# Expert loop of a mixture-of-experts block: three banks for up, two results in one bank, outputs copied by VectorE

## What is computed

```python
logits = jnp.einsum('th,eh->te', x, gate_w)
scores = jax.nn.softmax(logits, axis=-1)
topk_w, topk_idx = jax.lax.top_k(scores, K)                      # K = 2, E = 16
combine = jnp.sum(jax.nn.one_hot(topk_idx, E, dtype=x.dtype) * topk_w[..., None], axis=1)
gu = jnp.einsum('th,ehj->etj', x, w_gate_up)                     # H = 256, 2 * I = 352
h = _swiglu(gu, I)                                               # silu(g) * u
y = jnp.einsum('eti,eih,te->th', h, w_down, combine)
y = y + _swiglu(x @ shared_gate_up, SI) @ shared_down            # SI = 352
```

## Time and profile before

| | us |
|---|---|
| median of 3 runs (lowest, highest) | 277.54 (276.98, 279.88) |
| the profiled execution's own time | 279.51 |
| its span, first to last instruction | 277.7 |
| mean granted clock of TensorE, share of full | 0.981 |
| TensorE busy with matmuls, share of the span | 247.9, 89% |
| VectorE, ScalarE, GpSimd busy | 152.3, 125.7, 92.2 |

### The profile page before, as it was taken

The page is one execution under the profiler, slowest core; times in us unless marked ns, Lnnn a source line. Parts: engine busy times, 40 slices in busy tenths (PEclk is TensorE's granted clock), DMA queues, the critical chain, the costliest instruction groups (busy, mean ns, idle before and its releaser), DMA issues.

```text
span 277.7 us, 4961 instructions
## 1 busy us (share of the span) xinstructions
PE 247.9 (89%) x1518; PEld 173.9 (63%) x1518; DVE 152.3 (55%) x460; ACT 125.7 (45%) x461; POOL 92.2 (33%) x106
## 2 busy tenths in 40 slices
PE   3799899898989999988789999899988998798995
PEld 2455565565555667676668787567755765475784
DVE  1636658878888766535797598452202213121274
ACT  1164867759595778910334225033314323233430
POOL 2110110111111201011552005647566575575471
PEclk9999999999999999999799999999997999979999
DMA  7999977100000800000004000322232232333394
GB/s 216 267 333 372 333 173 182 54 2 1 1 2 3 294 1 4 0 2 0 0 4 145 4 0 5 96 76 83 89 94 67 84 97 78 94 79 77 99 362 162
DMA packets 20706, 28.02 MB, mean 101 GB/s; under 512 B 2688, under 2 KB 17674, under 8 KB 20682
## 3 DMA queue, kind: packets, MB, share of 16 engines
q1 hardware_dynamic: 16395, 18.71, 22.1%
q0 software_dynamic: 2976, 8.13, 10.1%
q10 hardware_dynamic: 1311, 0.88, 1.1%
HBM read 21.55 MB, written 6.16 MB: 100 GB/s over the span
## 4 chain that ended last, share of the span: by engine, by line
PE 69%; DVE 10%; issue 6%; ACT 6%; DMA 4%; another core or an unknown queue 3%; SPq 1%; POOL 0%; ACTq 0%; DVEq 0%; POOLq 0%
PE bank L874 14%; PE bank L886 8%; PE bank L805 8%; PE bank L547 5%; PE bank L506 5%; ACT pr_s L983 4%; PE bank L537 3%; DMA x_s<-in_x 3%; PE bank L559 3%; PE bank L582 3%; PE bank L865 3%; PE bank L855 2%; PE bank L528 2%; DVE kbd L1217 2%
## 5 line engine op out<-in xcount | busy, mean ns | idle before, releaser
L983 ACT ACTIVATE pr_s<-bank,mx 128x128 f32<-128x128 f32 x128 | 46.7, 421 | 2.6 <-DVE mx L1207 2.6
L874 PE MATMUL bank<-gu_s,bxT 128*128 x124 | 44.3, 483 | 1.9 <-DVE bxT L1520 1.7
L1526 DVE TENSOR_TENSOR pr_s<-bank,pr_s 128x176 f32<-128x176 f32 x31 | 10.6, 341 | 61.7 <-ACT pr_s L1146 47.0
L464 POOL DMA_INDIRECT expert_out<-by,prT x31 | 32.0, 1032 | 26.5 <-ACT by L973 20.5
L973 ACT ACTIVATE prT<-bank 128x512 f32<-128x512 f32 (+1 forms) x63 | 32.8, 521 | 16.9 <-PE bank L547 11.2
L459 POOL DMA_INDIRECT qx_s<-ffn_in,prT x31 | 30.1, 972 | 14.6 <-issue 9.3
L983 ACT ACTIVATION_READ_ACCUMULATOR pr_s<-bank,mx 128x1 f32 x128 | 33.6, 263 | 0.0
L886 PE MATMUL bank<-dn_s,prT 88*128 x124 | 32.5, 386 | 0.1
L874 PEld LDWEIGHTS bank<-gu_s,bxT 128*128 128x128 f32 x124 | 21.9, 196 | 10.4 <-issue 4.0
L973 ACT ACTIVATE by<-bank 128x256 f32<-128x256 f32 x31 | 11.9, 385 | 26.2 <-PE bank L886 10.9
L547 PE MATMUL bank<-tab,pr_s 128*128 128x128 f32 x128 | 20.2, 280 | 3.9 <-ACT pr_s L983 2.6
(11 more groups left out here) (186 smaller groups left out, 422.4 us busy)
## 6 DMA issues: line engine op xcount, KB each, us to landing
gu_s<-in_w_gu SPq DMA_DIRECT2D x8, 704.0 KB, 9.2
dn_s<-in_w_dn SPq DMA_DIRECT2D x4, 704.0 KB
qx_s<-in_ctx_in SPq DMA_DIRECT2D x2, 512.0 KB, 9.8
ffn_in<-x_s SPq DMA_DIRECT2D x4, 256.0 KB, 2.6
cv_s<-expert_out SPq DMA_DIRECT2D x4, 256.0 KB, 3.3
x_s<-expert_out SPq DMA_DIRECT2D x4, 256.0 KB, 4.8
out<-x_s SPq DMA_DIRECT2D x7, 128.0 KB
gu_s<-in_x_t SPq DMA_DIRECT2D x1, 768.0 KB, 12.1
```

Of the source, the lines that this page charges most:

```text
L464: pool.indirect_dma_start(expert_out[:], bass.IndirectOffsetOnAxis(ap=idx[:, 1, k:k + 1], axis=0), by[:, k % RB, :], None).then_inc(dma_sc ...
L874: last = mm(bank[2 + i % 2][:, 0:2 * I], bxT[:, i % 2, k, :], gu_s[:, k, bass.ds(e, 1), :], start=k == 0, stop=k == KD - 1)
L983: last = nc.scalar.activation(pr_s[:, n % 2, h, :], score_bank(n)[:, h * T:(h + 1) * T], ACT.Exp, bias=mx[:, n % 4, h:h + 1], accum_out=de ...
```

## The change

The loop is skewed by one block more. TensorE's iteration i is now hidden_transpose(i-3), expert_up(i), block_transpose(i+3), expert_down(i-4). Up has three banks (2, 3, 5) in place of two, the turned products keep two. The turned rows and the outputs share three banks (6, 7, 4), the rows in the first 256 columns and the outputs in the last 256: bank i mod 3 gets block_transpose(i+3) and then expert_down(i-4), and VectorE reads both after that. So bT_out(i+3) waits for expert_down(i-4) as well, block_transpose for the y_out of the outputs that were in its bank, and expert_down for bT_out. The turned rows (now blT, carved from prT), bh and bhT have three copies; bs has two still. y_out moves from ScalarE's list to VectorE's, behind h_mul(i) and bT_out(i+3); its last four stand ahead of weigh_pair(0). GpSimd's scatter is ten blocks behind its gather in place of eight. The last pair's shared matmuls use banks 5, 3, 5 in place of 5, 7, 6. Six registers hold expert numbers in place of four.

```diff
@@ -291,8 +292,12 @@
-        shared_bank = lambda q, c: bank[((6, 7, 1) if q < PAIRS - 1 else (5, 7, 6))[c]]
+        shared_bank = lambda q, c: bank[((6, 7, 1) if q < PAIRS - 1 else (5, 3, 5))[c]]
...
+        expert_bank = lambda i: bank[(2, 3, 5)[i % 3]]
+        row_bank = lambda i: bank[(6, 7, 4)[i % 3]]
+        out_rows = lambda i: row_bank(i + 7)[:, D:2 * D]
...
@@ -314,8 +319,9 @@
-        bh = carve(prr, 2 * I).rearrange("p (r n) -> p r n", r=2)
-        bhT = carve(ptr, 4 * T)[0:IH, :].rearrange("p (r k t) -> p r k t", r=2, k=2)
+        bh = carve(prr, 3 * I).rearrange("p (r n) -> p r n", r=3)
+        bhT = carve(ptr, 6 * T)[0:IH, :].rearrange("p (r k t) -> p r k t", r=3, k=2)
+        blT = carve(ptr, 3 * KD * T).rearrange("p (r k t) -> p r k t", r=3, k=KD)
...
@@ -449,7 +455,7 @@
-            LAG = RB + 4
+            LAG = RB + 6
...
             for i in range(BLOCKS + LAG):
@@ -460,7 +466,7 @@
-                    pool.wait_ge(act_expert_out, k + 1)
+                    pool.wait_ge(dve_expert_out, k + 1)
...
@@ -849,10 +855,14 @@
             def block_transpose(i):
...
                 pe.wait_ge(dma_gathered[slot], 16 * (i // RB) + 16)
-                if i >= 2:
-                    pe.wait_ge(dve_block_T, i - 1)
+                if i == 2:
+                    pe.wait_ge(dve_rows, 1)
+                if i >= 3:
+                    pe.wait_ge(dve_block_T, i - 2)
+                if i >= 10:
+                    pe.wait_ge(dve_expert_out, i - 9)
                 for k in range(KD):
-                    last = tr(bank[6 + i % 2][:, k * T:(k + 1) * T], bx[:, slot, k * 128:(k + 1) * 128], idf)
+                    last = tr(row_bank(i)[:, k * T:(k + 1) * T], bx[:, slot, k * 128:(k + 1) * 128], idf)
...
             def hidden_transpose(i):
@@ -862,39 +872,42 @@
                 for k in range(2):
-                    last = tr(hidden_bank(i)[0:IH, k * T:(k + 1) * T], bh[:, i % 2, k * IH:(k + 1) * IH], idf)
+                    last = tr(hidden_bank(i)[0:IH, k * T:(k + 1) * T], bh[:, i % 3, k * IH:(k + 1) * IH], idf)
...
             def expert_up(i):
...
-                if i >= 2:
-                    pe.wait_ge(dve_hidden, i - 1)
+                if i == 1:
+                    pe.wait_ge(dve_shared_added, 2)
+                if i == 2:
+                    pe.wait_ge(dve_shared_hidden, SC * (PAIRS - 1) + 1)
+                if i >= 3:
+                    pe.wait_ge(dve_hidden, i - 2)
                 for k in range(KD):
-                    last = mm(bank[2 + i % 2][:, 0:2 * I], bxT[:, i % 2, k, :], gu_s[:, k, bass.ds(e, 1), :],
+                    last = mm(expert_bank(i)[:, 0:2 * I], blT[:, i % 3, k, :], gu_s[:, k, bass.ds(e, 1), :],
...
             def expert_down(i):
...
                 pe.wait_ge(act_hidden_T, i + 1)
-                if i >= 2:
-                    pe.wait_ge(act_expert_out, i - 1)
-                if i == 1:
-                    pe.wait_ge(dve_shared_hidden, SC * (PAIRS - 1) + 1)
+                if i >= 3:
+                    pe.wait_ge(dve_expert_out, i - 2)
+                pe.wait_ge(dve_block_T, min(i + 5, BLOCKS))
                 for k in range(2):
-                    last = mm(bank[4 + i % 2][:, 0:D], bhT[:, i % 2, k, :], dn_s[:, k, bass.ds(e, 1), :],
-                              start=k == 0, stop=k == 1)
+                    last = mm(out_rows(i), bhT[:, i % 3, k, :], dn_s[:, k, bass.ds(e, 1), :],
+                              start=k == 0, stop=k == 1, skip_group_check=True)
...
             def read_expert(i):
...
             def expert(i):
...
@@ -933,26 +946,30 @@
-            for i in range(RB - 1):
+            for i in range(RB):
...
             block_transpose(1)
             expert_up(0)
-            pe.wait_ge(dve_shared_added, 2)
-            expert_up(1)
             block_transpose(2)
             block_transpose(3)
-            for i in range(2, BLOCKS):
-                hidden_transpose(i - 2)
+            expert_up(1)
+            block_transpose(4)
+            expert_up(2)
+            block_transpose(5)
+            for i in range(3, BLOCKS):
+                hidden_transpose(i - 3)
                 expert_up(i)
-                if i + 2 < BLOCKS:
-                    block_transpose(i + 2)
-                if i >= 3:
-                    expert_down(i - 3)
+                if i + 3 < BLOCKS:
+                    block_transpose(i + 3)
+                if i >= 4:
+                    expert_down(i - 4)
                 if i + 1 < BLOCKS:
                     read_expert(i + 1)
+            hidden_transpose(BLOCKS - 3)
+            expert_down(BLOCKS - 4)
             hidden_transpose(BLOCKS - 2)
             expert_down(BLOCKS - 3)
             hidden_transpose(BLOCKS - 1)
@@ -1143,33 +1160,23 @@
-                nc.scalar.activation(bs[:, i % 2, :], bank[2 + i % 2][:, 0:I], ACT.Silu).then_inc(act_expert_silu, 1)
+                nc.scalar.activation(bs[:, i % 2, :], expert_bank(i)[:, 0:I], ACT.Silu).then_inc(act_expert_silu, 1)
...
             def hT_out(i):
                 act.wait_ge(pe_hidden_T, i + 1)
-                if i >= 2:
-                    act.wait_ge(pe_expert_down, i - 1)
-                copy(bhT[:, i % 2, :, :].rearrange("p k t -> p (k t)"), hidden_bank(i)[0:IH, 0:2 * T]).then_inc(act_hidden_T, 1)
-            def y_out(i):
-                act.wait_ge(pe_expert_down, i + 1)
-                if i >= RB:
-                    act.wait_ge(dma_scattered[i % RB], 16 * (i // RB))
-                copy(by[:, i % RB, :], bank[4 + i % 2][:, 0:D]).then_inc(act_expert_out, 1)
+                if i >= 3:
+                    act.wait_ge(pe_expert_down, i - 2)
+                copy(bhT[:, i % 3, :, :].rearrange("p k t -> p (k t)"), hidden_bank(i)[0:IH, 0:2 * T]).then_inc(act_hidden_T, 1)
...
             silu(0)
             silu(1)
-            for i in range(2, BLOCKS):
-                hT_out(i - 2)
+            silu(2)
+            for i in range(3, BLOCKS):
+                hT_out(i - 3)
                 silu(i)
-                if i >= 3:
-                    y_out(i - 3)
-            hT_out(BLOCKS - 2)
-            y_out(BLOCKS - 3)
-            hT_out(BLOCKS - 1)
-            y_out(BLOCKS - 2)
-            y_out(BLOCKS - 1)
+            for i in range(BLOCKS - 3, BLOCKS):
+                hT_out(i)
...
@@ -1515,15 +1522,23 @@
             def bT_out(i):
                 dve.wait_ge(pe_block_T, i + 1)
-                if i >= 2:
-                    dve.wait_ge(pe_expert_up, i - 1)
-                V.tensor_copy(bxT[:, i % 2, :, :].rearrange("p k t -> p (k t)"), bank[6 + i % 2][:, 0:D]).then_inc(dve_block_T, 1)
+                if i >= 7:
+                    dve.wait_ge(pe_expert_down, i - 6)
+                if i >= 3:
+                    dve.wait_ge(pe_expert_up, i - 2)
+                V.tensor_copy(blT[:, i % 3, :, :].rearrange("p k t -> p (k t)"), row_bank(i)[:, 0:D]).then_inc(dve_block_T, 1)
+            def y_out(i):
+                dve.wait_ge(pe_expert_down, i + 1)
+                if i >= RB:
+                    dve.wait_ge(dma_scattered[i % RB], 16 * (i // RB))
+                V.tensor_copy(by[:, i % RB, :], out_rows(i)).then_inc(dve_expert_out, 1)
...
             def h_mul(i):
...
-                if i >= 2:
-                    dve.wait_ge(pe_hidden_T, i - 1)
-                V.tensor_tensor(bh[:, i % 2, :], bank[2 + i % 2][:, I:2 * I], bs[:, i % 2, :], ALU.mult).then_inc(dve_hidden, 1)
+                if i >= 3:
+                    dve.wait_ge(pe_hidden_T, i - 2)
+                V.tensor_tensor(bh[:, i % 3, :], expert_bank(i)[:, I:2 * I], bs[:, i % 2, :], ALU.mult).then_inc(dve_hidden, 1)
...
             def weigh_pair(t):
...
@@ -1537,16 +1552,23 @@
             shared_add(1)
             bT_out(1)
...
+            bT_out(2)
...
+            bT_out(3)
...
-            bT_out(2)
+            bT_out(4)
...
-            bT_out(3)
+            bT_out(5)
+            h_mul(2)
...
-            for i in range(2, BLOCKS):
+            for i in range(3, BLOCKS):
                 h_mul(i)
-                if i + 2 < BLOCKS:
-                    bT_out(i + 2)
+                if i + 3 < BLOCKS:
+                    bT_out(i + 3)
+                if i >= 4:
+                    y_out(i - 4)
+            for i in range(BLOCKS - 4, BLOCKS):
+                y_out(i)
             weigh_pair(0)
...
```

More of the change, by code:

```diff
@@ L47 @@
 RB = 4
+RE = 6
 PR = 4
@@ L242, in decoder_layer @@
         (pe_block_T, dve_block_T, pe_expert_up, act_expert_silu, dve_hidden, pe_hidden_T, act_hidden_T,
-         pe_expert_down, act_expert_out) = [sem(n) for n in (
+         pe_expert_down, dve_expert_out) = [sem(n) for n in (
             "pe_block_T dve_block_T pe_expert_up act_expert_silu dve_hidden pe_hidden_T act_hidden_T "
-            "pe_expert_down act_expert_out").split()]
+            "pe_expert_down dve_expert_out").split()]
         dma_token_outputs = [sem(f"dma_token_outputs{i}") for i in range(B)]
```

6 lines of the change are left out of this document (3 added, 3 removed).

## The result

| | before | after |
|---|---|---|
| median of 4 runs | 277.26 us (276.37 to 279.88) | 282.66 us (281.80 to 285.72) |
| ratio | | 1.020 (95%: 1.015 to 1.025) |
| profiled execution, its span | 279.51, 277.7 | 282.76, 280.9 |

The change makes the kernel slower by 2%, just outside the predicted range. The profiled execution of before was one of its longer ones, so the spans differ by 3.2 us where the medians differ by 5.4; what follows divides the 3.2, and the experiments repeat the division elsewhere.

The account below looks back on a forecast made before the run. The prediction took TensorE, at 2.49 us a block, to bound the kernel, with 11.8 us of the loop lost to late signals. Loop -4.3 and end +4.0 gave -0.3 on the 277.54 median: 277.2 us, range 270.5 to 281.5.

Parts of the forecast that it names:

- The bound and the period: Expert loop: TensorE is the engine to follow, its clean block stays 2.49 us, and the two added waits cost nothing.
- The room: Slack before TensorE needs a result: silu 2.7 to 5.2 us, bT_out 3.0 to 4.6, hidden_transpose to expert_down unchanged at 3.3.
- The loop keeps 7.5 and saves 4.3 us: Expert loop: of 11.8 us lost to late signals, 7.5 stay because GpSimd does not gain, and 4.3 are saved.
- four waits of 2.1, less the head start of about 1 us: GpSimd before its last gather: 8.4 us of waits after longer bursts, less about 1 us from the fuller prologue, leaving 7.5.
- rival C: Slower: GpSimd's bursts set the pace, the loop loses the 11.8 us again and late weighing costs 4: 281.5; chance 0.25.
- S: Mark near the kernel's end: when the last shared matmuls begin, as TensorE's last down matmuls end.
- The tail costs 4.0: Kernel end: VectorE's last four output copies stand before the weighing, costing 4.0 us, with ends of 3.0 and 5.2.
- The sum: Profiled span: 277.7 - 4.3 + 4.0 = 277.4 us; the difference of -0.3 put on the median gives 277.2.
- B: Stalls vanish: the loop saves 8 to 11.8 us, the end costs 3 to 5.2, say 271 us; chance 0.33.
- D: Depth has no effect, and VectorE's single row of waits chains the blocks: 282 to 284 us; chance 0.06.

Follow-up runs that it names:

- a2: The changed kernel run again unchanged, in a series without late signals: 275.27 us, ratio 1.031 to the kernel before.
- b2: The kernel before run again unchanged, in a series without late signals: 268.07 us, its middle 62.25 us.
- series 3: Runs made together on one chip that met the late signals; the kernel before took 275.78 us there, in a single run without a profile.
- m3b: The kernel before with each block's expert fixed, so TensorE reads no register, run again with late signals present: 277.91 us, where before took 275.78.
- series 0: The first pair of before and after, with late signals; all four runs of the kernel before took 276 to 280 us.
- e1: The changed kernel with only the last four output copies given back to ScalarE: 272.30 us, ratio 1.013 to the kernel before at 267.50.
- e2b: The deeper loop with every output copy on ScalarE, run again with late signals present: 281.56 us, where the kernel before took 275.78.
- e3: The kernel before, two-deep loop, with only its output copies moved to VectorE: 273.52 us, ratio 1.014 to the kernel before at 267.50.
- e2: The deeper loop alone, with every output copy on ScalarE: 268.79 us, ratio 1.007 to the kernel before at 267.50.
- n3b: The kernel before with plain SyncE stores for scatters and a 128x1024 GpSimd memset in each scatter's place, rerun: 267.47 us, where before took 279.70.
- n1: The kernel before with plain SyncE stores for scatters and a second 128-row gather in each scatter's place: 278.10 us, where before took 267.29.

## Why the prediction was wrong, point by point

- **The bound and the period**: right. 2.49 us a clean block before and after, the added waits free; no gap before hidden_transpose or expert_up any more, and no clock of 0.50 in the middle of the changed kernel (1.00, it was 0.95).
- **The room**: right in kind. The one step whose room stayed at 3.3 us, hT to down, is where the longest gaps went (1.68, 1.71, 1.34); the bursts grew from four blocks to five, as forecast; gather waits of 0.4 to 0.9 appeared between them.
- **The loop keeps 7.5 and saves 4.3 us**: mis-sized. The middle keeps 72.10 - 62.25 = 9.85, a saving of 1.9. Against the clean deep loop's 61.83 (a2) the late signals still cost 10.3 us, where they cost 11.8. The term that failed is "four waits of 2.1, less the head start of about 1 us". Before its last gather GpSimd has five waits in the changed kernel, of 2.85, 2.47, 2.82, 2.97 and 2.77 us. The first, at the start of the loop, is there in clean executions as well (2.04 in a2, 1.73 in b2). The other four come to 9.8 us when 0.30 is taken off each: the count was right, the length 2.5 in place of 2.1, and no part of the sum shows the head start. The 2.1 was also the longest of before, whose five waits behind late signals in this stretch average 1.9. So there are fewer bursts, but a longer wait behind each; over 68 us GpSimd idles 25.5 us for 24.4. This is rival C's reasoning, that GpSimd's bursts set the pace; the prediction saw it and gave C 0.25. Why the waits grow with the bursts was not shown. In series 3 the deep loops took 71.2 and 72.7; no profile of before stands beside them, but the two-deep m3b took 70.8, so that the saving of series 0 did not come again.
- **The fill**: missing. The deeper order turns the rows of one more block and multiplies them by the up weights ahead of block 2's hidden transposes: +1.6 us, given back in the loop, and in a2, e1 and e2b another 1.7 at the lower clock. The prediction has no term for this: it counts the fuller prologue only as a head start, and does not name the fourth register read. With the fill, S moves from 95.8 us behind the first gather to 94.3: 1.5 us saved in place of 4.3.
- **The tail costs 4.0**: mis-sized, by a choice. The two ends were 3.0 (the scatter of block 26 is no wait) and 5.2 (it is), and 4.0 lies between two outcomes of which one happens whole. The estimate of the scatter's issue, S - 3.2, was exact (262.73); its release came 5.9 us later, where the row gave 5.4, and the last shared_mul started at S + 9.7, not S + 9.5. (By the Trainium skill, DMA: Bandwidth & Descriptors, Anatomy of one DMA — SWDGE (gpsimd) path, whose fit gives an estimate of 2.3 us, there would have been no wait. b2's 31 scatters take 2.7 us from issue to landing in the median, near that; the scatter of block 26, beside the token loads, releases its copy only after 5.4 to 6.4 us in b2, before, after, e3 and a2. That it is the loads which slow it was not tested.) The tail cost 5.5. The forecast of 12 to 14 us from S to the end was 15.0.
- **What the depth does to the token loads**: missing. They start 1.5 us nearer to the end, and e1 and e2 pay 1.8 us for the depth alone. In the changed kernel the loads have landed before its weighing begins, and the depth's cost comes another way: block 26 is scattered nearer to S (3.2 us ahead of it in a2, 4.5 in e3), and the last y_out waits 3.46 us for it in place of 1.88, so that the weighing starts at S + 3.6 in place of S + 1.9.
- **The sum**: -4.3 + 4.0 = -0.3 forecast; -2.3 (S from 268.27 to 265.95, of which 0.8 is the earlier start) + 5.5 = +3.2 measured on the span. Of the named cases C is the nearest (1.5 us saved behind the first gather, where C decides below 1.2), with a tail of 5.5 in place of 4; the median of 282.66 lies over the range's end of 281.5. The medians differ by 5.4 and the spans by 3.2: before's profiled execution took 279.51 where its median is 277.26, and no profile divides the 2.2 us between.
- **Rivals B and D**: B fell (in the changed kernel the silu of block 14 still starts 5.0 us behind its up, where B's sign was that none starts more than 3 us behind), and so did D (no gap of the changed kernel stands before hidden_transpose, where a held-up h_mul would show; e2b, with none of them on VectorE, has a middle of 72.7).

## What to carry to other kernels

Here deeper buffers paid for late signals only up to the step that was not deepened, and cost a longer fill and a later last result; count the fill and the drain beside the loop. Before a copy moves to another engine, write out that engine's queue at the end of the kernel: what stands behind the copy there, and which transfer the copy waits for. When a stall's cause is not in the trace, run the unchanged kernel once more elsewhere before pricing a remedy for it: here 8 to 12 us of the loop were there in three series out of six and gone in the others.

## What the runs showed of the hardware that was not expected

- The same kernel takes 267.3 to 267.5 us in three series and 275.8, 277.3 and 279.7 in three others. Between the two profiled executions compared, before and b2, the loop differs by 11.8 us, and what differs in it is that TensorE's completions reach ScalarE and VectorE up to 5.0 us late while GpSimd writes indirect-DMA descriptors back to back (0.95 to 0.99 us a list of 128 rows, 0.30 us between lists). A memset of the same length did no such harm in the one execution that tested it (n3b).
- A second gather of 128 rows a block, with the plain stores, is more than the transfers keep up with: in n1, on a clean loop, gathers land late from block 28 on (0.15, 1.05 and 1.17 us of TensorE idle) and the tail grows from 9.2 to 13.3 us.
- A stop of 1.42 us for four register reads was followed by the 1.2 GHz level in three of six executions (L811 2.81, 3.65 and 2.85 us instead of 1.97); a stop of 1.06 us for three reads in none of twelve.
